# Value products moved from behind the third quarter of the deep tile to directly behind the scores, in a transformer layer on one core

## Chip, core and metric

The kernel runs on 1 core of one Trainium2 chip. The metric is the device time of one execution in microseconds (us), as the median of 3 runs. Engines are called TensorE (PE in the profile; its weight loads PEld), VectorE (DVE), ScalarE (ACT), GpSimd (POOL) and SyncE (SP, which issues all DMAs).

## What is computed

One pre-norm transformer layer over 8 sequences of 512 tokens and 256 features, in fp32:

```python
x = x + attention(layernorm(x))          # 16 heads of 16, rotary, masked softmax
x = x + ffn(layernorm(x))

# attention: key j is seen by query i if j <= i and
#   (same block of 64) or (i < 4 or j < 4) or |i - j| <= 128
attn = softmax(where(mask, q @ k.T * scale, min)); out = (attn @ v) @ out_w.T

# ffn, 256 -> 1024 -> 1024 -> 1024 -> 256
h = silu(x @ w1.T * s1) * (x @ w2.T * s2)
h = gelu(h @ h1.T * t1)
h = gelu(h @ h2.T * t2)
y = h @ w3.T * s3
```

## The kernel before

Each engine runs its own program, in order; semaphores tie them. Work goes in rounds r = -1 to 7. Round r first runs the gated part of the feed-forward network of sequence r (16 half tiles, line 642), then `beside_attention(r)`: 20 steps n = 0 to 19, in which the two deep layers and the down projection of sequence r are interleaved with the attention of sequence a = r + 1 and the projections of sequence b = r + 2. Round -1 has only attention and projections; round 7 only the feed-forward network; rounds 0 to 6 have attention and deep tiles, and rounds 0 to 5 projections too.

A deep tile is one 128x512 output tile of a layer of 1024 by 1024: 8 blocks of weights, each times a high and a low part of the input, so 16 matmuls (line 671), in one of two banks. `deep_quarter` issues 4 of them. Steps 0 to 15 have one deep tile each, steps 16 to 19 one tile of the down projection (line 695).

Attention goes in 16 units of 4 heads by 128 queries; unit n has query tile i = n // 4 and head group g = n % 4. A unit goes through a pipeline over the steps:

- Step n: `scores` on TensorE (line 541, 4 matmuls of 64 rows, two halves of the array, banks 2 and 3), then on VectorE mask and minimum (line 995, 4 operations), on ScalarE the exponentials (line 813, 4 operations).
- Step n + 2 (`T_LAG`): `turn_cur` (line 553) and `turn_prev` (line 561, not for the first query tile) transpose the probabilities of the own and of the previous block of keys, into banks 5 and 4. VectorE copies the one (`keep_cur`, line 1010), ScalarE the other (`keep_prev`, line 820), into a ring of two buffers `PT`.
- Step n + 3 (`PV_LAG`): `weighted_values` (line 584), products of 32 output rows each, 8 for the first query tile and 16 for the others, all in bank 7. It waits for both copies of its unit. The first unit of a query tile (g = 0) also waits for `pv_kept`, the signal that `keep_heads` on VectorE (lines 1015 and 1017) has taken the query tile before out of bank 7. The last (g = 3) adds the products with the global keys (line 593) and transposes the inverse sums (line 597); it waits for `rinv_spread` and `glob_kept`.

VectorE's order in a step is: `keep_sum` of the deep tile of the step before (line 1046, it waits for that tile's last matmul), `rotary` of the projection issued in the step before (lines 941 and 942, steps 4 to 7), `keep_heads` (steps 7, 11, 15, 19), the minimum of this step's unit, `keep_cur`, `inverse_sums`, `residual` (line 1026). ScalarE's order is: exponentials of this step's unit, `keep_prev` of the unit two before, then GELU of finished deep tiles in steps 4, 6, 7 and 12, 14, 15 (lines 833 and 834, and its rest at the start of steps 8 and 16), with table loads on the way there and back. On TensorE the projections (line 491, steps 3 to 6), `global_scores` (line 502, step 8), `out_projection` (line 607, steps 7, 11, 15, 19) and `turn_globals` (line 568) stand at the end of a step, or in steps 16 and 17 ahead of the down tile, as do the transposes for the second normalization (line 616).

SyncE issues the load of the next weights when a deep tile is done, and the loads of stacked queries and keys.

Of the kernel before, what the change touches and what calls it, by code (L numbers as in the profile page):

```python
# [30 lines left out]
UNITS = NT * HEADS // UH  # L31
# [42 lines left out]
def wait(engine, semaphore, value):  # L74
    if value > 0:
        engine.wait_ge(semaphore, value)


def layer_kernel(nc, x, qkvT, outT, ffn_w, ffn_s, s3row, rope, mask, small, out):
# [23 lines left out]
    with ctx:  # L103
# [193 lines left out]
        def has_a(r):  # L297
            return r + 1 < NB

        def has_q(r):  # L300
            return r + 2 < NB
# [149 lines left out]
        def _(pe):  # L451
# [75 lines left out]
            def scores(a, n):  # L527
                i, g = n // GROUPS, n % GROUPS
                if g == 0:
                    pe.wait_ge(stacked[i], 16 * LOADS * (a + 1))  # L530
                if n:
                    pe.wait_ge(s_free, HALVES * a + 2 * n)
                elif a:

                    pe.wait_ge(mul_done, GATED * a)
                lo = 0 if i else P
                for half in range(2):
                    for c2 in range(2):
                        rows = slice(half * PARTS * HD, (half + 1) * PARTS * HD)
                        pair = g * UH // 2 + c2  # L540
                        mm = nc.tensor.matmul(bank[2 + half][:, c2 * KEYS + lo:(c2 + 1) * KEYS],  # L541
                                              Qs[rows, pair, i % 2, :],
                                              Ks[rows, pair, i * P + lo - P:(i + 1) * P], start=True, stop=True)
                    mm.then_inc(s_done, 1)

            def turn_cur(a, n):
                pe.wait_ge(exp_done, UNITS * a + n + 1)
                if n:
                    pe.wait_ge(cur_kept, UNITS * a + n)
                else:  # L550
                    pe.wait_ge(v_kept, 2 * NT * (a + 1))
                for c in range(UH):
                    mm = nc.tensor.transpose(bank[5][:, c * P:(c + 1) * P], unit_scores(n, P)[:, c, :], ident)  # L553
                mm.then_inc(cur_turned, 1)

            def turn_prev(a, n):
                if n < GROUPS:
                    return
                wait(pe, prev_kept, LATER * a + n - GROUPS)
                for c in range(UH):  # L560
                    mm = nc.tensor.transpose(bank[4][:, c * P:(c + 1) * P], Sm[:, n % SM_RING, c, 0:P], ident)  # L561
                mm.then_inc(prev_turned, 1)
# [8 lines left out]
            def weighted_values(a, n):  # L571
                i, g = n // GROUPS, n % GROUPS
                f = g * UH // HPT
                pe.wait_ge(cur_kept, UNITS * a + n + 1)
                if i:
                    pe.wait_ge(prev_kept, LATER * a + n - GROUPS + 1)
                if g == 0:
                    wait(pe, pv_kept, NT * a + i)
                out = bank[7][:, f * P:(f + 1) * P]
                v = (v_even, v_odd)[g % 2]  # L580
                for side in ((1, 0) if i else (1,)):
                    for c in range(UH):
                        col = f * P + 32 * c
                        mm = nc.tensor.matmul(out[32 * c:32 * c + 32, :], v[:, i - 1 + side, col:col + 32],  # L584
                                              PT[:, n % 2, side, c, :], start=(g == 0 and side == 1),
                                              stop=(g == GROUPS - 1 and side == (0 if i else 1) and i < 2),
                                              skip_group_check=True)
                if g == GROUPS - 1:
                    if i > 1:
                        pe.wait_ge(vg_kept, a + 1)  # L590
                        pe.wait_ge(glob_kept, 2 * a + i - 1)
                        for f in range(NF):
                            mm = nc.tensor.matmul(bank[7][:, f * P:(f + 1) * P], Vg[:, f * P:(f + 1) * P], PgT[:, :],
                                                  start=False, stop=(f == NF - 1), skip_group_check=True)
                    pe.wait_ge(rinv_spread, NT * a + i + 1)
                    for f in range(NF):
                        mm = nc.tensor.transpose(  # L597
                            bank[7][:, EMB + f * P:EMB + (f + 1) * P],
                            rinv_wide[:, f * HPT:(f + 1) * HPT, :].rearrange("p h d -> p (h d)"), ident)
                mm.then_inc(pv_done, 1)  # L600
# [46 lines left out]
            def deep_quarter(r, n, quarter, general):  # L647
                layer, m = n // NH, n % NH
                h_hi, h_lo = ((a_hi, a_lo), (b_hi, b_lo))[layer]
                if quarter == 0:  # L650
                    if n == 0:
                        pe.wait_ge(mul_done, GATED * (r + 1))
                    elif n >= 2:
                        pe.wait_ge(sum_kept, DEEP * r + n - 1)
                    if m in DN_SLOTS:
                        pe.wait_ge(w_loaded[m], 16 * (3 * r + 1 + layer))
                    elif m in UP_SLOTS:
                        pe.wait_ge(w_loaded[m], 16 * (3 * r + 2 + layer))
                    else:
                        pe.wait_ge(w_loaded[m], 16 * (2 * r + 1 + layer))  # L660
                for kk in (2 * quarter, 2 * quarter + 1):
                    if n == 0:
                        pe.wait_ge(up_split, GATED * r + NH + kk + 1)
                    if n == NH:
                        pe.wait_ge(deep_split, DEEP * r + kk + 1)
                    lhsT = W[:, m, kk * P:(kk + 1) * P]
                    for part, h in enumerate((h_hi, h_lo)):
                        rhs = h[:, kk, :]
                        if general:
                            rhs = rhs.bitcast(F32)  # L670
                        mm = nc.tensor.matmul(bank[n % 2][:, :], lhsT.bitcast(F32) if general else lhsT, rhs,  # L671
                                              start=(kk == 0 and part == 0), stop=(kk == NH - 1 and part == 1))
                if quarter == 3:
                    mm.then_inc(deep_done, 1)
# [25 lines left out]
            def step(r, n, general):  # L700
                a, with_a, with_q, with_f = r + 1, has_a(r), has_q(r), r >= 0
                t, u = n - T_LAG, n - PV_LAG
                if with_a and n < UNITS:
                    scores(a, n)
                if with_f and n < DEEP:
                    deep_quarter(r, n, 0, general)
                if with_a and 0 <= t < UNITS:
                    turn_cur(a, t)
                if with_f and n < DEEP:
                    deep_quarter(r, n, 1, general)  # L710
                if with_a and 0 <= t < UNITS:
                    turn_prev(a, t)
                if with_a and n == UNITS:
                    ln2_transposes(r, 0)
                if with_a and n == UNITS + 1:
                    turn_globals(r, 1)
                if with_f and n < DEEP:
                    deep_quarter(r, n, 2, general)
                if with_a and 0 <= u < UNITS:
                    weighted_values(a, u)  # L720
                if with_f and n < DEEP:
                    deep_quarter(r, n, 3, general)
                if with_f and n >= DEEP:
                    down_tile(r, n - DEEP, general)
                if with_q and n in LN1_STEPS:
                    ln1_transposes(r, n - LN1_STEPS[0])
                if with_q and 0 <= n - QK_STEP < 2 * NF:
                    qk_projection(r, n - QK_STEP)
                if with_q and n == GS_STEP:
                    global_scores(r)  # L730
                if with_a:
                    if (i := tile_at(n, 7)) is not None:
                        out_projection(r, i)
                    if n == 13:
                        turn_globals(r, 0)
                    if n in (UNITS + 1, UNITS + 2):
                        ln2_transposes(r, n - UNITS)
# [613 lines left out]
```

## Time and profile before

| what | value |
|---|---|
| median of 3 runs | 1212.31 us (1211.03 to 1213.5) |
| profiled execution, its own time | 1214.82 us |
| its span, first to last instruction | 1212.9 us |
| TensorE busy | 1115.3 us, 92% of the span |
| its weight loads | 852.9 us, 70% |
| ScalarE / VectorE / GpSimd busy | 720.7 / 634.8 / 456.6 us |
| mean granted clock of TensorE | 0.965 |
| chain that ended last | TensorE 85%, of which line 671 41% |

Busy time of matmuls is modelled and overlapping instructions are counted together, so start times say more of TensorE than durations. The first 163 us hold loads of the inputs, the first projections and the attention of sequence 0; from 183 us on a round takes 138.8 us.

### The profile page before, as it was taken

The numbers are of one execution on the slowest core, as the hardware profiler recorded it, in microseconds if no ns is written. First come the engines' busy times: TensorE is split into PE (matmuls) and PEld (weight loads), VectorE is DVE, ScalarE is ACT, GpSimd is POOL, SyncE is SP. The second block draws the span as 40 slices with busy tenths as digits, with TensorE's granted clock in tenths as the row PEclk, the third lists the DMA queues.
The fourth block names the chain that finished last, engine by engine and source line by source line (L and its number), as shares of the span: only waits on it lengthen the run. The fifth ranks groups of instructions, "written<-read, shape, count | busy, mean of one in ns | idle before, by whom it ended". The sixth has DMA issues, their size and how long they took to land.

```text
span 1212.9 us, 21563 instructions
## 1 busy us (share of the span) xinstructions
PE 1115.3 (92%) x7538; PEld 852.9 (70%) x7538; DVE 634.8 (52%) x1979; ACT 720.7 (59%) x1780; POOL 456.6 (38%) x646
## 2 busy tenths in 40 slices
PE   4465879999999999999999999999999999999998
PEld 1333566777867787677867788677877788777887
DVE  3254535754556545654556545665556544554422
ACT  1256745865656844856657745757557655856422
POOL 5131132722444333624525324624427223324433
PEclk9676789999999999999999999999999999999999
DMA  8797476555447255564546463565356454531540
GB/s 246 249 346 230 133 219 188 176 167 147 159 140 242 78 168 160 164 199 122 169 128 218 131 168 129 175 208 139 110 169 201 129 157 143 149 109 54 174 139 18
DMA packets 157470, 198.54 MB, mean 164 GB/s; under 512 B 7601, under 2 KB 116401, under 8 KB 157361
## 3 DMA queue, kind: packets, MB, share of 16 engines
q1 hardware_dynamic: 157360, 197.13, 53.2%
q8 instruction: 63, 1.03, 0.4%
q14 instruction: 47, 0.38, 0.1%
HBM read 155.16 MB, written 49.28 MB: 169 GB/s over the span
## 4 chain that ended last, share of the span: by engine, by line
PE 85%; SPq 5%; DVE 3%; ACT 2%; issue 2%; DMA 2%; POOL 1%; POOLq 0%; ACTq 0%; DVEq 0%
PE bank L671 41%; PE bank L642 10%; PE bank L695 5%; PE bank L584 5%; PE bank L553 4%; PE bank L541 4%; PE bank L491 4%; PE bank L561 3%; PE bank L607 2%; PE bank L515 2%; DMA qk_scratch<-split 2%; SPq L317 1%; SPq L332 1%; SPq L351 1%; PE bank L597 1%
## 5 line engine op out<-in xcount | busy, mean ns | idle before, releaser
L813 ACT ACTIVATE Sm<-Sm,smin 128x260 f32<-128x260 f32 (+2 forms) x512 | 241.4, 473 | 217.5 <-DVE smin L995 217.0
L671 PE MATMUL bank<-b_hi,W 128*128 128x512 f32 x512 | 222.4, 434 | 0.2 <-POOL b_lo L1227 0.2
L671 PE MATMUL bank<-a_hi,W 128*128 128x512 f32 x512 | 215.1, 420 | 1.1 <-DVE a_act L1070 1.1
L671 PE MATMUL bank<-b_lo,W 128*128 128x512 f32 x512 | 201.4, 393 | 0.0
L671 PE MATMUL bank<-a_lo,W 128*128 128x512 f32 x512 | 200.7, 392 | 0.0
L1046 DVE TENSOR_SCALAR a_sum<-bank,scales 128x512 f32<-128x512 f32 x64 | 48.1, 751 | 166.8 <-PE bank L671 166.8
L642 PE MATMUL bank<-x_hi,W 128*128 128x256 f32 x512 | 127.0, 289 | 7.0 <-issue 7.0
L642 PE MATMUL bank<-x_lo,W 128*128 128x256 f32 x512 | 125.4, 286 | 0.0
L1236 POOL TENSOR_TENSOR a_lo<-a_act,a_hi 128x256 fp32r<-128x256 f32 x128 | 94.0, 737 | 83.3 <-ACT a_hi L864 83.3
L995 DVE CUSTOM_DVE_ANT_0 Sm<-bank,msk,gmin 128x256 f32<-128x256 f32 x256 | 108.4, 480 | 16.6 <-PE bank L541 16.6
L671 PEld LDWEIGHTS bank<-b_hi,W 128*128 128x128 f32 x512 | 96.2, 188 | 28.7 <-issue 7.1
L671 PEld LDWEIGHTS bank<-a_hi,W 128*128 128x128 f32 x512 | 96.1, 188 | 27.9 <-issue 5.6
L1227 POOL TENSOR_TENSOR a_lo<-a_act,a_hi 128x512 fp32r<-128x512 f32 x64 | 80.9, 1289 | 85.0 <-ACT a_hi L834 85.0
L1046 DVE TENSOR_SCALAR b_sum<-bank,scales 128x512 f32<-128x512 f32 x64 | 48.1, 751 | 119.9 <-PE bank L671 119.9
L671 PEld LDWEIGHTS bank<-a_lo,W 128*128 128x128 f32 x512 | 96.5, 189 | 15.2
L642 PEld LDWEIGHTS bank<-x_hi,W 128*128 128x128 f32 x512 | 99.7, 195 | 9.4 <-issue 9.4
L671 PEld LDWEIGHTS bank<-b_lo,W 128*128 128x128 f32 x512 | 96.8, 189 | 12.3
L1227 POOL TENSOR_TENSOR b_lo<-b_act,b_hi 128x512 fp32r<-128x512 f32 x64 | 83.9, 1335 | 48.3 <-ACT b_hi L834 48.3
L1154 POOL TENSOR_SCALAR ve<-mv 128x1 f32<-128x1 f32 x64 | 14.2, 223 | 229.2 <-DVE mv L1030 202.8
L642 PEld LDWEIGHTS bank<-x_lo,W 128*128 128x128 f32 x512 | 99.8, 195 | 0.0
L1070 DVE SCALAR_TENSOR_TENSOR a_act<-bank,scales,silu 128x256 f32<-128x256 f32 x128 | 62.0, 484 | 72.1 <-ACT silu L870 71.9
L541 PEld LDWEIGHTS bank<-Ks,Qs 64*128 64x128 f32 x512 | 40.6, 193 | 84.1 <-issue 54.7
(106 smaller groups left out, 2229.1 us busy)
## 6 DMA issues: line engine op xcount, KB each, us to landing
W<-w_scratch SPq DMA_DIRECT2D x176, 512.0 KB, 3.9
qk_scratch<-split SPq DMA_DIRECT2D x128, 256.0 KB
Qs<-qk_scratch SPq DMA_DIRECT2D x64, 256.0 KB, 5.2
Ks<-qk_scratch SPq DMA_DIRECT2D x64, 256.0 KB, 5.4
w_scratch<-in_ffn_w SPq DMA_DIRECT2D x22, 512.0 KB, 7.0
x_in<-in_x SPq DMA_DIRECT2D x8, 512.0 KB, 7.4
x<-in_x SPq DMA_DIRECT2D x8, 512.0 KB, 4.1
stage_a<-in_ffn_w SPq DMA_DIRECT2D x8, 512.0 KB, 8.0
```

What stands on the lines that cost most here:

```text
L491: mm = nc.tensor.matmul(MISC[:, :], qkv_w[:, kk, col:col + P], xnT[:, kk, :], start=(kk == 0), stop=(kk == NF - 1))
L541: mm = nc.tensor.matmul(bank[2 + half][:, c2 * KEYS + lo:(c2 + 1) * KEYS], Qs[rows, pair, i % 2, :], Ks[rows, pair, i * P + lo - P:(i + 1) ...
L584: mm = nc.tensor.matmul(out[32 * c:32 * c + 32, :], v[:, i - 1 + side, col:col + 32], PT[:, n % 2, side, c, :], start=(g == 0 and side == ...
L642: mm = nc.tensor.matmul(bank[DOWN_BANKS[s % 4]][:, u * HALF:(u + 1) * HALF], lhsT.bitcast(F32) if general else lhsT, rhs, start=(kk == 0 a ...
L671: mm = nc.tensor.matmul(bank[n % 2][:, :], lhsT.bitcast(F32) if general else lhsT, rhs, start=(kk == 0 and part == 0), stop=(kk == NH - 1 ...
L695: mm = nc.tensor.matmul(bank[DOWN_BANKS[t]][:, 0:EMB], lhsT, rhs.bitcast(F32) if general else rhs, start=(kk == 0 and part == 0), stop=(kk ...
L813: ex = nc.scalar.activation(row, row, ACT.Exp, bias=smin[:, r, c:c + 1], scale=-1.0, accum_out=rowsum[:, i % 2, col:col + 1])
L995: tt = nc.vector.tensor_tensor_reduce(out=unit_scores(n, lo)[:, c, :], in0=bank[2 + half][:, c2 * KEYS + lo:(c2 + 1) * KEYS], in1=msk[:, i ...
L1046: nc.vector.tensor_scalar((b_sum, a_sum)[layer][:, m, :], bank[n % 2][:, :], scales[:, 2 + layer, m:m + 1], None, ALU.mult).then_inc(sum_k ...
L1070: nc.vector.scalar_tensor_tensor(a_act[:, m, half * HALF:(half + 1) * HALF], bank[DOWN_BANKS[s % 4]][:, HALF:SEQ], scales[:, 1, m:m + 1], ...
L1227: nc.gpsimd.tensor_tensor(lo[:, m, :], full[:, m, :], hi[:, m, :].bitcast(F32), ALU.subtract)\
L1236: nc.gpsimd.tensor_tensor(a_lo[:, m, cols], a_act[:, m, cols], a_hi[:, m, cols].bitcast(F32), ALU.subtract).then_inc(up_split, 1)
```

## The change

In each step `weighted_values` of unit n - 3 is issued directly behind the scores of unit n and ahead of the first deep quarter. Before it stood between the third and the fourth quarter. In steps 16 and 17 it thereby also goes ahead of the transposes, in step 18 it stays where it was. Nothing else moves: the other engines' programs, the waits and the buffers are the same.

```diff
                 t, u = n - T_LAG, n - PV_LAG
                 if with_a and n < UNITS:
                     scores(a, n)
+                if with_a and 0 <= u < UNITS:
+                    weighted_values(a, u)
                 if with_f and n < DEEP:
                     deep_quarter(r, n, 0, general)
                 if with_a and 0 <= t < UNITS:
...
                 if with_f and n < DEEP:
                     deep_quarter(r, n, 2, general)
-                if with_a and 0 <= u < UNITS:
-                    weighted_values(a, u)
                 if with_f and n < DEEP:
                     deep_quarter(r, n, 3, general)
```

## Rows read from the trace of the kernel before

**Rows 1.** Granted clock by slices (page), and busy time in steps 0 to 10, round 2

```profile
PEclk9676789999999999999999999999999999999999
...
core 0: us, PE busy (x) PEld busy (x) DVE busy (x) ACT busy (x) POOL busy (x), PEclk, DMA share, GB/s
460.00:528.00 68.00, 67.20 (x406) 47.86 (x406) 43.12 (x146) 44.40 (x117) 31.04 (x41) 1.00 0.63 191
```

**Rows 2.** Chain of waits, round 2, steps 4 and 11: start us, us, what

```profile
483.87 1.84 PE bank L671 x8
...
529.88 1.12 PE bank L671 x4
...
531.44 0.93 PE bank L671 x4
...
533.73 0.57 PE bank L584 x16
534.31 1.13 PE bank L671 x4
```

**Rows 3.** Timeline of TensorE, attention-only stretch: start, us, engine, line [idle before <- releaser]

```profile
124.60 0.64 PE L584 MATMUL bank<-PT,v_odd 128*32 128x128 f32 x16
125.17 0.51 PE L541 MATMUL bank<-Ks,Qs 64*128 64x256 f32 x4
125.61 0.66 PE L553 MATMUL bank<-consts,Sm 128*128 128x128 f32 x4
```

**Rows 4.** Timeline of TensorE: scores of steps 7, 9, 10, 11, 12, 14

```profile
503.55 0.51 PE L541 MATMUL bank<-Ks,Qs 64*128 64x256 f32 x4
...
517.18 0.50 PE L541 MATMUL bank<-Ks,Qs 64*128 64x256 f32 x4
...
523.18 0.51 PE L541 MATMUL bank<-Ks,Qs 64*128 64x256 f32 x4
...
529.37 0.51 PE L541 MATMUL bank<-Ks,Qs 64*128 64x256 f32 x4
529.81 0.50 PE L671 MATMUL bank<-b_hi,W 128*128 128x512 f32 x1
...
536.23 0.51 PE L541 MATMUL bank<-Ks,Qs 64*128 64x256 f32 x4
...
548.29 0.51 PE L541 MATMUL bank<-Ks,Qs 64*128 64x256 f32 x4
```

**Rows 5.** Timeline of TensorE, attention-only stretch: two waits for ScalarE

```profile
119.66 0.66 PE L561 MATMUL bank<-consts,Sm 128*128 128x128 f32 x4 [1.73 <-ACT PT L820]
...
128.37 1.12 PE L561 MATMUL bank<-consts,Sm 128*128 128x128 f32 x4 [2.10 <-ACT PT L820]
```

**Rows 6.** Timeline of VectorE, steps 7 and 11 of round 2

```profile
503.65 0.69 DVE L941 TENSOR_TENSOR k<-bank,cos_sin 128x512 f32<-128x512 f32 x1 [0.96 <-PE bank L491]
...
505.35 0.42 DVE L1017 TENSOR_TENSOR featT<-bank,inv_sum 128x256 f32<-128x256 f32 x1
...
529.48 0.75 DVE L1046 TENSOR_SCALAR a_sum<-bank,scales 128x512 f32<-128x512 f32 x1 [3.22 <-PE bank L671]
...
530.60 0.42 DVE L1017 TENSOR_TENSOR featT<-bank,inv_sum 128x256 f32<-128x256 f32 x1
```

**Rows 7.** Timeline of ScalarE, steps 8, 9 and 12 to 13

```profile
517.07 0.56 ACT L820 COPY PT<-bank 128x512 f32<-128x512 f32 x1
...
521.57 0.56 ACT L820 COPY PT<-bank 128x512 f32<-128x512 f32 x1
...
538.61 0.51 ACT L813 ACTIVATE Sm<-Sm,smin 128x260 f32<-128x260 f32 x1 [3.38 <-DVE smin L995]
...
546.22 1.28 ACT L813 ACT_TABLE_LOAD   x1
...
549.52 0.56 ACT L820 COPY PT<-bank 128x512 f32<-128x512 f32 x1
```

**Rows 8.** Timelines of VectorE and TensorE, step 16 of round 1

```profile
424.34 0.41 DVE L1026 TENSOR_TENSOR x<-x,bank 128x256 f32<-128x256 f32 x1
...
424.81 0.44 PE L616 MATMUL bank<-consts,xn 128*128 128x128 f32 x2 [0.68 <-DVE x L1026]
```

## The prediction

> **What bounds the kernel now.** I read the engine summary of the page, then the busy time by stretch, then the chain of waits through one round, and last the start times of single instructions. The stretches show TensorE busy for 67.20 of 68 us in steps 0 to 10 of round 2, at full granted clock [rows 1]. The chain of waits there is TensorE and nothing else [rows 2]. So in a step that holds a deep tile, whatever lengthens TensorE's queue lengthens the program, one for one, and whatever shortens it is won, as long as nothing it needs comes late. The change does both.
>
> **What a block of small tiles costs TensorE.** A step interleaves the deep tile (16 matmuls that use the whole array) with score products (64-row tiles), two sets of transposes and value products (32-column tiles). In the chain, four deep matmuls behind a transpose take 0.93 us; behind the value products they take 1.13 us; eight in one piece take 1.84 us where no transposes or values stand between them [rows 2]. So the cut that the values make between the third and fourth quarter costs 0.93 + 1.13 - 1.84 = 0.22 us beside the values' own 0.57 us. The scores show the same exit price already (1.12 us for the four behind them), and keep it or hand it on to the values. If scores and values stand together, one such crossing into and out of the whole array goes. What the new boundary, scores to values, costs is not in the trace, but the opposite one is: in the attention-only stretch the values start at 124.60, the scores behind them at 125.17, the transposes at 125.61, so 0.57 and 0.44 us from start to start [rows 3]. That is what values take ahead of the whole array (0.57) and scores ahead of it (529.37 to 529.81, 0.44) [rows 2, 4]. So the boundary adds nothing of its own, and hides nothing. I take 0.21 us saved per step. Bounds: 0 if this order of the two pays a crossing of its own, 0.65 if the scores (0.44) ran entirely under the values.
>
> The Trainium skill says the same of the mechanism ("TensorEngine Tiling (Array Packing)", Key Properties): a change of tiling mode drains TensorE. By it the step goes from four changes of mode to three, since 64-row and 32-column tiles are two modes; the rows' 0.22 us is such a drain, and the sum by rule and row is equal. The rule only denies the case where the two sets overlap.
>
> It counts in steps 3 to 15, in rounds 0 to 6, which have both a deep tile and attention: 13 x 7 = 91 times 0.21 = **19.1 us gained**. Steps 16 to 18 have no deep quarters. There the values get whole-array neighbours on both sides before and after the change, so no crossing goes: 0. In round 7 there are no values. In the attention-only stretch TensorE waits for ScalarE anyway, 1.73 and 2.10 us at single transposes [rows 5]; the values now go ahead of the transposes instead of behind them, and ScalarE's exponentials, 2 us a step, lie over that. I take 0, with 3 us either way.
>
> **What the values wait for, and how late it is.** Moved, they would start 0.44 us behind the start of the scores of their step, instead of some 4.3 us behind it (529.37 to 533.73). What they need:
>
> *The copy of the finished heads, in steps 7, 11 and 15.* There the values begin a new query tile in bank 7, and wait for VectorE's L1017. VectorE gets to it only behind keep_sum, which waits for the last matmul of the tile just before, so no speed-up elsewhere helps. In step 11 keep_sum starts at 529.48 and L1017 at 530.60, done at 531.02; the values could start at 529.81: 1.21 us late [rows 4, 6]. Step 15 has the same order. In step 7 the rotary pair of the last projection stands between: L941 at 503.65, waiting for that projection, and L1017 at 505.35, done at 505.77, against 503.55 + 0.44 = 503.99: 1.78 us [rows 4, 6]. Round 6 has no rotary, so 1.21 there. Sum: 6 x 1.78 + 1.21 + 14 x 1.21 = 28.8 us.
>
> *The copy of the previous block's transposes, every step from 7.* ScalarE makes it (L820) behind the exponentials of the next step but one, and behind GELU parts. For step 14 it is late: exponentials of step 12 start at 538.61, then run on without a break through the GELU of four tiles and its table loads (the way back at 546.22), the next exponentials, and L820 at 549.52, done at 550.08. The scores of step 14 start at 548.29, so the values could start at 548.73: 1.35 us late [rows 4, 7]. That chain starts from the scores of step 12 (536.23), and two steps of TensorE get 0.21 us shorter each, so 1.77 us; x 7 = 12.4 us. Step 9 looks critical too: done at 517.63 against 517.62 [rows 4, 7]. But its ScalarE chain starts in step 7, ahead of the new stall of 1.78 us, which pushes only TensorE; two shorter steps take 0.42 back and 1.3 us of slack are left. In step 10 it is done at 522.13 against 523.62, 1.49 us early [rows 4, 7]; one shorter step leaves over 1.2. Steps 5, 6 and below need no late copy, 8, 12 and 13 stand like 10.
>
> *Resuming.* TensorE starts about 0.06 us after the awaited end: the add at 424.34 takes 0.41, the transpose starts at 424.81 [rows 8]. 28 waits x 0.06 = 1.7 us.
>
> Behind a waiting value product on TensorE stand all four quarters of the deep tile, ready; they wait too. The scores stand ahead of it, so the VectorE minimum and ScalarE's exponentials start as before. SyncE's weight loads wait for the end of deep tiles; they come later with them, with nothing new queued. No instruction or DMA is added.
>
> **Sum:** -19.1 + 28.8 + 12.4 + 1.7 = +23.8 us. The profiled execution took 1214.82 us over a span of 1212.9, 2.5 us above the median of the runs (1212.31); so I expect a span near 1237 and a median near **1236**. Three stalls of heads and one of the copy cost about 6.2 us a round, the saved crossings return 2.7.
>
> **Rivals.**
> 1. *The copy for step 14 isn't late* (ScalarE's chain moves with something I don't see). For: in steps 10 and 13 it has slack. Against: ScalarE runs without a gap from 538.61 to 550.08. 23.8 - 12.4 - 0.4 = +11: 1223.
> 2. *Scores to values pays its own crossing.* Then no gain and 1.35 at step 14: 28.8 + 9.4 + 1.7 = +40: 1252. Against: rows 3 in the other order.
> 3. *The clock falls in the new waits.* In the attention-only stretch, the transposes behind a wait of 1.73 us still show 0.66 us, those behind 2.10 show 1.12 [rows 5]. The new waits are up to 1.8 us, but each amid 6 us of dense work, at granted clock 1.00 [rows 1]. If each cost another 1.5 us: 24 + 28 x 1.5 = +66: 1278.
> 4. *Faster: scores and values overlap in the array.* This saves up to 0.65 us x 91 = 59 against 43 of waits (41.2 of lateness and 1.7 of resuming): -16, 1196. It decides from 43 / 91 = 0.47 us a step. Against: the values and scores of rows 3 stand one behind the other at full price.
> 5. *The waits hold nothing up,* since the deep matmuls go ahead of the waiting values: -19: 1193. Against: at 424.81 TensorE idled 0.68 us for a transpose [rows 8] while the value products behind it, whose copies were long there, did not start. The Trainium skill ("TensorE: Matmul & The Clock Gate", Part 2) says that only weight loads are pulled ahead and matmuls keep program order; the row agrees.
>
> **Chances.** My forecast 0.70; rival 1 0.10; rival 2 0.08; rival 3 0.04; rival 4 0.04; rival 5 0.01; waits and gains that happen to cancel 0.03. Own spread of the forecast: saved crossing 0.15 to 0.25 (5 us each way), step 14 at 1.35 to 1.9 (3 us), attention-only stretch 3 us: 1228 to 1244. The range for 8 in 10 takes in rival 1 and part of rival 2: 1220 to 1247. About 0.2% (2.4 us) is what a measurement of this kernel can tell from no change: faster 0.05, same 0.03, slower 0.92.
>
> **What would show it.** In the changed profile: values 0.57 us, directly behind the scores, and no TensorE gap in steps 4, 5, 6, 8, 9, 10, 12, 13; eight deep matmuls in 1.84 us where third and fourth quarter meet; TensorE idle for L1017 in 7 (1.8 us), 11 and 15 (1.2 us each), and for L820 in 14 (1.8 us); rounds 3.4 us longer. I am wrong if the first four deep matmuls behind the values take over 1.13 us, if scores to values takes other than 0.44 us, if the gap in 14 is missing, or if new gaps turn up in 8 to 10, from a ScalarE chain that I took as fixed.

## Result and the profile after

The changed kernel takes 1258.66 us (median of 4, 1256.05 to 1260.21) against 1212.9 (median of 4): 3.7% slower, ratio 1.0373, interval 1.036 to 1.0387. The prediction was 1236, range 1220 to 1247: the sign was right, the size about half of what came. The profiled execution took 1256.05 us over a span of 1254.1, 41.2 us longer than before. Page of the changed kernel, busy times, granted clock by slices, and engines of the chain:

```profile
PE 1103.7 (88%) x7538; PEld 868.3 (69%) x7538; DVE 634.2 (51%) x1979; ACT 724.5 (58%) x1780; POOL 455.8 (36%) x646
...
PEclk9686889999999899999999899999999999999999
...
PE 75%; ACT 8%; DVE 6%; SPq 4%; issue 3%; DMA 2%; POOL 1%; POOLq 0%; ACTq 0%; DVEq 0%
```

TensorE works less (1103.7 us instead of 1115.3) in a longer span, and the chain goes over ScalarE for 8% of it and VectorE for 6% (2% and 3% before). In the rounds, where the clock line of [rows 1] has nothing but nines, it has an 8 in slices 14 and 23. A slice is 31 us long, so 3.3 us at half clock leave its mean at 0.95, which still prints as a 9: the line shows only the two longest stretches at half clock.

Chain of waits of the changed kernel, step 11 of round 2 (start us, us, what; it answers to [rows 2]):

```profile
543.07 0.75 DVE a_sum L1046
543.82 0.34 DVE inv_sum L1015
544.16 0.02 issue
544.19 0.44 DVE featT L1017
544.62 0.14 issue
544.76 0.64 PE bank L584 x16
545.40 1.13 PE bank L671 x4
...
548.34 1.86 PE bank L671 x8
550.20 0.86 PE bank L607 x4
```

Both halves of the forecast stand here. The third and fourth quarters are one piece (1.86 us instead of 0.93 and 1.13), and ahead of the values the chain leaves TensorE for keep_sum and the copy of the heads. It comes back 0.14 us after the copy, where I had put 0.06.

Timelines of the changed kernel, round 2, TensorE in steps 7, 11 and 14 and ScalarE's late copy (they answer to [rows 4] and [rows 7]):

```profile
514.47 0.51 PE L541 MATMUL bank<-Ks,Qs 64*128 64x256 f32 x4
516.83 0.85 PE L584 MATMUL bank<-PT,v_even 128*32 128x128 f32 x16 [1.86 <-DVE featT L1017]
517.62 0.79 PE L671 MATMUL bank<-a_hi,W 128*128 128x512 f32 x1
518.21 0.63 PE L671 MATMUL bank<-a_lo,W 128*128 128x512 f32 x1
518.63 0.63 PE L671 MATMUL bank<-a_hi,W 128*128 128x512 f32 x1
...
521.14 0.39 PE L671 MATMUL bank<-a_lo,W 128*128 128x512 f32 x1
...
544.76 0.64 PE L584 MATMUL bank<-PT,v_even 128*32 128x128 f32 x16 [1.29 <-DVE featT L1017]
...
562.70 0.51 PE L541 MATMUL bank<-Ks,Qs 64*128 64x256 f32 x4
564.99 0.64 PE L584 MATMUL bank<-PT,v_odd 128*32 128x128 f32 x16 [1.78 <-ACT PT L820]
```

```profile
564.28 0.56 ACT L820 COPY PT<-bank 128x512 f32<-128x512 f32 x1
```

The waits are where they were forecast. Counted as in the prediction, from the start of the scores plus 0.44, they are 1.92 us in step 7 (1.35 in round 6), 1.36 in 11 and 15, and 1.85 in 14 (564.99 - 562.70 - 0.44), apart from step 7 the same in all seven rounds. They hold the time to resume. What wasn't forecast stands behind the wait of step 7: the deep matmuls there start 0.42 us apart (518.21 to 518.63) instead of 0.23 (1.84 / 8). Busy time and granted clock of the changed kernel around it (columns as in [rows 1]):

```profile
514.00:517.00 3.00, 1.14 (x14) 0.50 (x16) 2.38 (x8) 2.98 (x4) 2.48 (x2) 1.00 0.50 193
517.10:520.40 3.30, 3.30 (x25) 2.43 (x14) 0.96 (x6) 2.51 (x9) 3.22 (x4) 0.51 0.75 263
520.60:524.00 3.40, 3.40 (x18) 2.82 (x18) 1.42 (x3) 1.97 (x3) 0.42 (x1) 1.00 0.27 69
```

The granted clock went to half, 1.2 GHz, just behind the wait, for at least these 3.3 us, and back. Before the fall TensorE had been busy for 1.14 of 3 us. Such a stretch at half clock is called a fall below. In step 14 of round 1 it was about twice as long (its slice of the clock line has an 8):

```profile
418.00:425.00 7.00, 7.00 (x35) 5.54 (x27) 0.69 (x1) 1.88 (x8) 1.07 (x3) 0.51 0.05 18
```

To see where this happened I took the length of each step, from scores to scores, in both profiles. Change of the length in us, after less before:

| round | steps 3 to 6 | 7 | 8 to 10 | 11 | 12, 13 | 14 | 15 to the next scores |
|---|---|---|---|---|---|---|---|
| 0 | -0.83 | 1.74 | -0.63 | 1.18 | -0.35 | 1.64 | 1.08 |
| 1 | -0.81 | 1.73 | -0.66 | 1.15 | -0.35 | **4.75** | 1.06 |
| 2 | -0.81 | **3.29** | -0.62 | 1.18 | -0.35 | 1.64 | 1.23 |
| 3 | -0.81 | 1.73 | -0.63 | 1.15 | -0.35 | **4.75** | 1.07 |
| 4 | -0.85 | **3.28** | -0.63 | 1.15 | -0.35 | **3.15** | 1.07 |
| 5 | -0.85 | **3.34** | -0.63 | 1.16 | -0.35 | **3.20** | 1.08 |

Round 6 has 1.18 in step 7 and 1.63 in 14. Each of steps 3 to 14 without a wait is 0.15 to 0.26 us shorter, and each with one is longer by the forecast amount within 0.12 us (wait and resuming less the crossing: 1.63 in step 7, 1.06 in 11, 1.62 in 14), but for seven steps (bold) that are 1.5 to 1.6 us, or, at the two 4.75, 3.1 us longer again. The stretch up to the first step of round 0 is 1.0 us longer.

### The profile page after: what moved, and what is told of

It reads as the page before. It is cut to its first block, busy times and chain, and to the rows that moved or that the text cites. A ratio compares the mean times of both kernels' runs of the same rounds, so it can differ in the third digit from the quotient of the medians.

```text
span 1254.1 us, 21563 instructions
## 1 busy us (share of the span) xinstructions
PE 1103.7 (88%) x7538; PEld 868.3 (69%) x7538; DVE 634.2 (51%) x1979; ACT 724.5 (58%) x1780; POOL 455.8 (36%) x646
## 4 chain that ended last, share of the span: by engine, by line
PE 75%; ACT 8%; DVE 6%; SPq 4%; issue 3%; DMA 2%; POOL 1%; POOLq 0%; ACTq 0%; DVEq 0%
PE bank L671 35%; PE bank L642 9%; PE bank L695 5%; PE bank L584 4%; PE bank L553 4%; PE bank L491 4%; PE bank L541 3%; ACT Sm L813 3%; PE bank L561 2%; PE bank L607 2%; PE bank L515 2%; DMA qk_scratch<-split 2%; SPq L332 1%; ACT a_act L833 1%; SPq L351 1%
## 5 line engine op out<-in xcount | busy, mean ns | idle before, releaser
L671 PE MATMUL bank<-b_hi,W 128*128 128x512 f32 x512 | 219.7, 429 | 0.2 <-POOL b_lo L1227 0.2
L1010 DVE COPY PT<-bank 128x512 f32<-128x512 f32 x128 | 88.4, 691 | 108.0 <-PE bank L553 107.7
```

The lines of the kernel that those rows point to most:

```text
L1010: nc.vector.tensor_copy(PT[:, n % 2, 1, :, :].rearrange("p c q -> p (c q)"), bank[5][:, :])\
```

## Experiments

Medians of the kernel before, run beside these kernels, were 1212.3 to 1213.4 us.

**The crossing alone, and the shorter waits alone.** In the first two kernels `weighted_values` is behind the scores only in some steps of rounds 0 to 6:

```diff
+                early = with_f and n < 7              # second kernel: n in (11, 15)
+                if with_a and 0 <= u < UNITS and early:
+                    weighted_values(a, u)
                 if with_f and n < DEEP:
                     deep_quarter(r, n, 0, general)
...
-                if with_a and 0 <= u < UNITS:
+                if with_a and 0 <= u < UNITS and not early:
                     weighted_values(a, u)
```

> Only steps 3 to 6 of rounds 0 to 6 have the value products behind the scores; there every copy they need is done 1.1 to 4.7 us before, so nothing waits. Theory A (the crossing is saved, waits and clock cost the rest): 28 steps x 0.21 = 5.9 us faster than before, 1206.5. Theory B (scores to values pays its own crossing, so nothing is saved): within 1 us of before. No step shows a granted clock under 1.00 from 183 us on.

Measured: 1206.96 us, ratio 0.9953 (0.9939 to 0.9966), 6.4 us faster. Step by step the profile gives -0.19 to -0.23 in steps 3 to 6 of all seven rounds and changes within 0.04 elsewhere. The boundary from scores to values pays no crossing of its own and hides nothing; rivals 2 and 4 are out.

> Only steps 11 and 15 of rounds 0 to 6 are moved (the waits for the copy of the heads, 1.21 us of lateness and 0.15 us of resuming each, as the changed kernel shows). Theory A (the clock falls only behind the longer waits of steps 7 and 14): 14 x (1.36 - 0.21) = 16 us slower than before, 1229, clock 1.00 throughout the rounds. Theory B (every new wait can lower the clock): 20 us slower or more, half clock behind some of the 14 waits.

Measured: 1228.68 us, ratio 1.0132 (1.0116 to 1.0147), 15.3 us slower; steps 11 and 15 are 1.13 to 1.18 us longer, in every round. Round 2 of this kernel, busy time and granted clock:

```profile
460.00:599.00 139.00, 133.62 (x926) 102.45 (x926) 78.36 (x245) 87.73 (x218) 55.35 (x79) 1.00 0.52 160
```

The clock is 1.00 here, and no step in any other round is longer than its wait says: fourteen waits of 1.36 us brought no fall. These waits cost their length and no more.

**The longer waits, with steps 7 and 14 moved alone** (`n in (7, 14)`):

> Only steps 7 and 14 of rounds 0 to 6 are moved. Lateness: step 7 6 x 1.78 + 1.21, step 14 7 x 1.35 (steps 12 and 13 are no shorter here), resuming 14 x 0.15, saved 14 x 0.21: +20.5 us from the waits alone. Theory A (the clock falls behind waits of 1.8 us, by chance of timing): +20.5 and 1.7 us for each fall of 3.4 us length, 3 to 9 of them: 26 to 36 us slower, 1239 to 1249, with half clock behind some of these waits. Theory B (the missing 22 us come from elsewhere): 20 us slower, clock 1.00.

Measured: 1242.98 us, ratio 1.0243 (1.0227 to 1.0259), 29.6 us slower; 9 us above the waits alone. No step 7 is longer than its wait says (1.71 to 1.75), but step 14 is 2.84 to 2.87 us longer in rounds 0 to 5, and 1.25 in round 6. Its wait is 1.49 us in all seven rounds. Timeline of TensorE in this kernel, step 14 of round 2, and the stretch behind it:

```profile
560.69 0.64 PE L584 MATMUL bank<-PT,v_odd 128*32 128x128 f32 x16 [1.42 <-ACT PT L823]
...
562.58 0.63 PE L671 MATMUL bank<-b_lo,W 128*128 128x512 f32 x1
563.00 0.63 PE L671 MATMUL bank<-b_hi,W 128*128 128x512 f32 x1
```

```profile
562.30:565.50 3.20, 3.20 (x11) 2.58 (x10) 0.55 (x1) 0.94 (x4) 0.00 (x0) 0.50 0.00 0
```

The shorter of the two waits is the one that lowers the clock, so my theory that the length decides was too simple. I separated the two later (below).

**The same waits with TensorE busy.** The change, and ahead of the waiting values of steps 7 and 14 six matmuls into the bank that the first quarter then overwrites:

```diff
+            def filler(r, n, general):
+                layer, m = n // NH, n % NH
+                pe.wait_ge(sum_kept, DEEP * r + n - 1)
+                pe.wait_ge(w_loaded[m], 16 * (2 * r + 1 + layer))
+                lhsT, rhs = W[:, m, 0:P], (a_hi, b_hi)[layer][:, 0, :]
+                for _ in range(6):
+                    nc.tensor.matmul(bank[n % 2][:, :], lhsT.bitcast(F32) if general else lhsT,
+                                     rhs.bitcast(F32) if general else rhs, start=True, stop=True)
...
+                if with_f and n in (7, 14):
+                    filler(r, n, general)
                 if with_a and 0 <= u < UNITS:
                     weighted_values(a, u)
```

> The change, and ahead of the waiting value products of steps 7 and 14 six more matmuls of 128x512 into the deep tile's bank, which the tile's first quarter then overwrites (1.4 us of work that isn't part of the computation). The value products still start no earlier than their copies allow. Theory A (the idle time lowers the clock): the waits are the same length, but TensorE works through them, the falls of the clock behind them go, and the kernel is 12 to 18 us faster than the changed one, 1241 to 1247, although it does 84 matmuls more. Theory B (the steps are long for another reason, or the clock falls whatever TensorE does there): 1257 to 1262 or more.

Measured: 1248.99 us, ratio 1.0299 (1.0282 to 1.0317): 9.7 us faster than the changed kernel, with 96 matmuls more. I had overlooked that the filler also runs in round 7, where no wait hides it; there it costs 2.7 us (from the last scores to the end of the profile 115.1 against 112.4). Less that, the kernel would stand at 1246.3, in the range of theory A; as measured it is 2 us above it. Timeline of TensorE of this kernel, step 7 of round 2, and its steps 0 to 10:

```profile
513.20 0.51 PE L541 MATMUL bank<-Ks,Qs 64*128 64x256 f32 x4
513.63 1.66 PE L682 MATMUL bank<-a_hi,W 128*128 128x512 f32 x6
515.57 0.64 PE L584 MATMUL bank<-PT,v_even 128*32 128x128 f32 x16 [0.27 <-DVE featT L1028]
516.14 0.50 PE L671 MATMUL bank<-a_hi,W 128*128 128x512 f32 x1
516.48 0.40 PE L671 MATMUL bank<-a_lo,W 128*128 128x512 f32 x1
```

```profile
471.30:540.00 68.70, 68.43 (x418) 50.35 (x418) 42.05 (x145) 44.23 (x115) 30.85 (x41) 1.00 0.64 200
```

The values start as long after the scores as in the changed kernel (515.57 - 513.20 = 2.37 against 516.83 - 514.47 = 2.36), but the deep matmuls behind them run at full clock. Each step 7 of rounds 0 to 5 is now 1.73 to 1.76 us longer than before and each step 14 1.64 or 1.65: all bold entries of the table are gone, and rounds 0 to 6 together are 13.8 us shorter than in the changed kernel (943.7 against 957.5 us from the first scores to those of step 15 in round 6). The mean granted clock of all four executions of the filled kernel is 0.965 to 0.968, that of the changed kernel's four 0.954 to 0.958. So the falls come with TensorE idling, and cost that much. One doubt is left: where the falls come also changes from kernel to kernel (the six unfilled waits of 1.92 us with steps 7 and 14 moved alone had none), so the filler may have removed some of them by moving the rounds in time rather than by its work.

**Heads first.** The change, with `keep_heads` ahead of `keep_sum` on VectorE:

```diff
+                    if with_a and n < UNITS and (i := tile_at(n, 7)) is not None:
+                        keep_heads(a, i)
                     if with_f and 0 <= n - 1 < DEEP:
                         keep_sum(r, n - 1)
...
-                        if (i := tile_at(n, 7)) is not None:
+                        if n >= UNITS and (i := tile_at(n, 7)) is not None:
                             keep_heads(a, i)
```

> The change, and on VectorE the copy of the finished heads ahead of keep_sum and the rotary pair instead of behind them in steps 7, 11 and 15. It then runs while VectorE idles, before the scores of the step. Theory A: the 21 waits for it go (28.8 us and 21 x 0.15), with the falls of the clock behind step 7; left are the wait in step 14 (7 x 1.92 = 13.4) and its clock falls (2 to 8 us) against 19.1 saved: 4 us faster to 2 us slower than before, 1209 to 1215. Theory B (bank 7 or something else makes the values late in these steps): over 15 us slower still.

Measured: 1222.54 us, ratio 1.0084 (1.0069 to 1.01): 36.1 us faster than the changed kernel, still 9.2 slower than before, and slower than I expected. Steps 7, 11 and 15 have no wait left (-0.17 to -0.19, -0.18 to -0.20, and 0.03 to 0.05 from step 15 up to the next round). The miss is in step 14: 3.19 to 3.23 us longer in all of rounds 0 to 5, so each of these six waits of 1.85 us was followed by a fall, 6 x 1.6 = 9.6 us, where I had allowed 2 to 8. Attention-only stretch and the wait in step 9 of rounds 5 and 6 (0.19 and 0.85 where rounds 0 to 4 have -0.21) give the rest.

**All but the late steps.** The change except in steps 7, 11, 14 and 15:

> The change in all steps except 7, 11, 14 and 15, where the value products stay behind the third quarter. Theory A (crossings saved where nothing is late): 9 steps x 7 rounds x 0.21 = 13.2 us saved, less 0.2 to 0.4 us in each step 9, which loses its slack (ScalarE's chain there starts in step 7, and no wait in step 7 holds TensorE back now): 11 us faster than before, 1202, no fall of the clock. Theory B (the values stand badly behind the scores in every step): not faster than the 5.9 us that steps 3 to 6 gave.

Measured: 1205.52 us, ratio 0.9934 (0.992 to 0.9949), 7.6 us faster; less than the 11 expected. The other eight steps are 0.15 to 0.26 us shorter, but step 9 is 0.09 or 0.10 longer in rounds 0 to 5, which is the loss of 0.3 us that was expected there, and 0.63 longer in round 6, which was not. Rounds 0 to 6 together are 10.3 us shorter in the profile. The rest is the attention-only stretch, changed here too: with the 2.8 us that the next kernel gives for it, 7.5 us remain.

**The attention-only stretch alone** (`early = not with_f`):

> The change in the attention-only stretch alone (round -1). Theory A (ScalarE and the transfers set that stretch): within 2 us of before, 1211 to 1215. Theory B (part of the missing time lies there, since the stretch reads 2.4 us longer in the changed kernel's profile): 2 to 5 us slower.

Measured: 1215.95 us (12 runs) against 1213.13, ratio 1.0025 (1.0014 to 1.0036), 2.8 us slower. I had put 0 there. Single profiles price this stretch badly. From its first scores to those of round 0 it reads 127.7 to 130.7 us in seven profiles whose values stand as before (130.4 in the kernel before itself), and 130.1 to 134.7 in the five with the change in it, in whole or in part. Waits of TensorE in that stretch of this kernel (us in total, times, longest):

```profile
PE bank L584 <- ACT PT L823: 15.5, 6, 7.1
...
PE bank L584 <- DVE featT L1020: 2.8, 1, 2.8
...
PE bank L593 <- ACT PgT L830: 1.4, 1, 1.4
```

and of VectorE for the transposes:

```profile
DVE PT L1013 <- PE bank L553: 14.5, 10, 5.0
```

In the kernel before VectorE waited 2.9 us in all for `turn_cur` there, and TensorE 13.0 us for ScalarE's copy, at the transposes (line 561). Now the transposes of a unit stand behind values that wait for ScalarE, and VectorE behind the transposes. That this is what makes the 2.8 us I argue from these waits; it was not tried. The single wait of 2.8 us for the copy of the heads (L1020 in this kernel) is new too, and is as good a candidate.

**Values one place later.** Values and scores together, but the values of unit n - 4 directly ahead of the scores of unit n:

```diff
+                if with_a and 0 <= n - 4 < UNITS:
+                    weighted_values(a, n - 4)
                 if with_a and n < UNITS:
                     scores(a, n)
```

> Values and scores stand together, but the values one place later than in the kernel before instead of earlier: the values of unit n - 4 directly ahead of the scores of unit n. Theory A (what the change wins is the crossing, what it loses is the time ahead of the awaited copies): 12 steps x 7 rounds x 0.21 = 17.6 us saved and no new wait, 1196, clock 1.00 throughout the rounds. Theory B (values and scores together disturb the step in another way, or the later values hold up the copies into their two buffers): no more than 5 us faster.

Measured: 1203.16 us, ratio 0.9918 (0.9903 to 0.9932), 10 us faster. No wait came, but three crossings a round that I had counted as saved are not: steps 6, 10 and 14 change by -0.03, -0.03 to -0.05 and -0.02 in rounds 0 to 5. The chain of waits of this kernel at step 7 of round 2 shows why:

```profile
496.76 0.36 PE bank L584 x8
497.12 0.37 PE bank L597 x2
497.49 0.44 PE bank L541 x4
...
503.57 0.57 PE bank L584 x16
504.15 0.44 PE bank L541 x4
```

The last unit of a query tile ends with transposes of the inverse sums (L597), which use the whole array and here come between the values and the scores.

**One longer wait a round,** to tell length from place:

> Only step 7 of rounds 0 to 6 moved: one wait a round, of 1.92 us in rounds 0 to 5 and 1.36 in round 6. Waits less crossings: 6 x 1.92 + 1.36 - 7 x 0.2 = +11.5 us. If the length of a wait decides on the clock, it falls here in most rounds (1.7 us for each fall of 3.4 us, up to +22); if it is decided by when in the round the wait comes, as steps 7 and 14 moved together suggest (no fall in step 7, a fall in step 14 in six of seven rounds), few falls or none: 11.5 us slower, 1225.

> Only step 14 of rounds 0 to 6 moved: one wait a round of 1.35 + 0.15 = 1.5 us, 7 x (1.5 - 0.2) = +9 us without the clock. If the length decides, fewer falls than in the kernel with step 7 alone: 9 to 12 us slower, 1222 to 1225. If the place decides, a fall in most rounds: 7 x 1.6 more, 20 us slower, 1233.

Measured: step 7 alone 1227.63 us, ratio 1.0125 (1.0109 to 1.014), 15.3 slower; step 14 alone 1223.36, ratio 1.0092 (1.0078 to 1.0106), 11 slower. In the first, rounds 1 and 4 have 3.33 us in step 7 and the others 1.71 or 1.72 (round 6, with its shorter wait, 1.18); in the second, rounds 1 and 6 have 2.87 and 2.84 in step 14 and the others 1.26 or 1.27. Waits followed by a fall, by the step lengths of the one profiled execution of each kernel:

| wait | kernel | falls |
|---|---|---|
| 1.36 us | steps 11 and 15 alone; changed kernel, the same steps | 0 of 14; 0 of 14 |
| 1.49 us, step 14 | alone; with step 7 | 2 of 7; 6 of 7 |
| 1.85 us, step 14 | changed kernel; heads first | 4 of 7; 6 of 7 |
| 1.92 us, step 7 | alone; with step 14; changed kernel | 2 of 6; 0 of 6; 3 of 6 |
| 1.85 and 1.92 us, filled | filled waits | 0 of 13 |

The same wait in the same step brings a fall in nearly every round of one kernel and in two of seven in another. Length alone doesn't decide, and neither does the step; what does was not settled.

**Combined.** Heads first, and values behind the scores in rounds 0 to 6 in all steps but 14:

> The copy of the heads ahead of keep_sum on VectorE, and the value products behind the scores in rounds 0 to 6 in every step but 14; the attention-only stretch keeps the old order of the values. Theory A (only lateness and clock turn the saved crossings into a loss): 12 steps x 7 rounds x 0.19 = 16 us saved, less the wait in step 9 of rounds 5 and 6 (0.6 and 1.05 us with the heads first): 14 us faster than before, 1199, clock 1.00 from 183 us on. Theory B: no faster than the variant that left steps 7, 11, 14 and 15 alone (1205.5).

Measured: 1198.34 us, ratio 0.9888 (0.9873 to 0.9903): 14 us faster than before, 60 faster than the changed kernel. Chain of waits, steps 11 and 12 of round 2:

```profile
520.73 0.44 PE bank L541 x4
521.16 0.57 PE bank L584 x16
521.74 1.12 PE bank L671 x4
...
524.67 1.85 PE bank L671 x8
526.51 0.86 PE bank L607 x4
527.38 0.44 PE bank L541 x4
527.81 0.57 PE bank L584 x16
```

In step 11, which begins at 520.73, the values of a new query tile follow the scores after 0.43 us; the copy of the heads holds them up no longer. Step 9 of round 6 is 0.84 us longer than before; in round 5, where 0.6 us of wait were expected, there is none.

## Why the prediction was wrong in size

- *Crossings saved, 91 x 0.21 = 19.1 us:* right. Steps 3 to 6 alone gave 6.4 us for 28 steps; the profile gives 0.15 to 0.26 a step. "TensorEngine Tiling (Array Packing)" of the Trainium skill (Key Properties) has a drain at every change of tiling mode; the whole-array transposes between values and scores, which brought the cost back in three steps of the later variant, agree with it.
- *Late heads, 28.8 us, and the late copy in step 14, 12.4 us:* right, place and size: 2.36 - 0.44 - 0.14 = 1.78 in step 7, 1.85 in step 14 with the resuming in it (1.77 + 0.14 would be 1.91). With them rivals 1 and 5, which had no wait in step 14 or none at all, are out.
- *Resuming, 0.06 us:* off; 0.14 in the chain. I read it from a transpose that waited for VectorE. 28 x 0.08 = 2.2 us more.
- *Slack in step 9:* right. No wait there in any round; when the heads no longer waited, step 9 of round 6 became 0.85 us longer.
- *Attention-only stretch, 0 with 3 us either way:* 2.8 us, at the edge of the bound. I argued that TensorE waits for ScalarE anyway, and did not follow what is queued behind the waiting values: the transposes, and VectorE behind these.
- *The clock:* here the prediction failed. Rival 3 named it; I gave it 0.04 and put the term at nothing in the sum, since the waits stand amid dense work at granted clock 1.00. That rows show 1.00 where there were hardly any waits says nothing of the clock once there are; the two waits of [rows 5] (1.73 us with fast transposes, 2.10 with slow ones) had the new ones near and between them, and should have given it a third or more. It cost 13.8 us in the profiled execution, and 12.4 in the medians (1258.66 less 1246.3, which would have been inside the range of 1220 to 1247). Rival 3 had the price of one fall right (1.5 us against 1.6), but put it behind all 28 waits; in the profile it came behind 7 of them.

The profiled execution adds up: 23.8 forecast, 2.2 for resuming, 13.8 for the clock, 1.0 ahead of round 0, together 40.8 of 41.2. In the medians, with 2.8 for the attention-only stretch, it is 23.8 + 2.2 + 12.4 + 2.8 = 41.2 of 45.8. The other 4.6 us are open. The changed kernel's profiled execution lies 2.6 us below its median and that of the kernel before 1.9 above its own, and runs of one kernel lie up to 6 us apart (1212.72 to 1218.67 in the attention-only kernel). The mean granted clocks of the changed kernel's unprofiled runs (0.954 to 0.957, profiled 0.958) point to more falls there, which was not shown.

## What to carry to other kernels

Blocks of small tiles put side by side save a crossing, 0.2 us here, but moving one forward in an in-order queue spends the slack of everything it waits for; subtract the end of each awaited copy from the new start, step by step, before moving it. Where one step is late, leave it, or move the copy ahead on its own engine instead: here the same idea lost 46 us in every step at once, and won 14 with the late step left out and the copy of the heads moved ahead. And price a new idle stretch of TensorE as its length plus a possible half-clock stretch behind it, even where the kernel before runs at full clock throughout.

## What was unexpected of the hardware

Waits of TensorE of 1.5 to 1.9 us between dense work were followed, in 23 of 46 cases, by half clock for some 3.3 us, worth 1.6 us each (at two of them for some 7 us, worth 3.1), and waits of 1.36 us in none of 28. Which of the longer ones it is was the same round after round in some kernels (step 14, six rounds in a row) and changed when another wait in the round was added or removed. Thirteen of these waits filled with matmuls brought none.
